# Where the decays' exponential is taken: per head from the broadcast row on ScalarE, with the causal mask moved to GpSimd

## What is computed

```python
log_fg = log_sigmoid(fgate)                      # gates come from q, k, v by a small matmul
cums = cumsum(log_fg);  fg_mat = cums[:, None] - cums[None, :]     # -inf above the diagonal
log_D = fg_mat + ig;    D = exp(log_D - max(log_D, -1))
C = (q @ k.T) / sqrt(128) * D
h = (C / (max(|sum(C)|, exp(-max_log_D)) + eps)) @ v               # then a norm per head
x = x + h * outnorm_weight
# feed-forward, BitNet style: act_quant(layernorm(x)) with ternary weights
x = x + bitlinear(silu(bitlinear(x, w_gate)) * bitlinear(x, w_up), w_down)
```

## Time and profile before

| | |
|---|---|
| median of 3 runs | 690.28 us (690.03 to 692.08) |
| span of the profiled execution | 685.3 us (its own time from launch to end is not given) |
| TensorE, VectorE busy | 85%, 83% of the span |
| ScalarE, GpSimd busy | 70%, 42% |
| mean granted clock of TensorE | 0.962 of full |

### The profile page before, as it was taken

The page is one execution under the profiler, slowest core; times in us unless marked ns, Lnnn a source line. Parts: engine busy times, 40 slices in busy tenths (PEclk is TensorE's granted clock), DMA queues, the critical chain, the costliest instruction groups (busy, mean ns, idle before and its releaser), DMA issues. The chain is left out here.

```text
span 685.3 us, 12637 instructions
## 1 busy us (share of the span) xinstructions
PE 579.8 (85%) x3568; PEld 377.8 (55%) x3630; DVE 567.8 (83%) x1518; ACT 476.5 (70%) x716; POOL 284.6 (42%) x459
## 2 busy tenths in 40 slices
PE   1824567889998999899998999799989999799996
PEld 1814555466555655476556656576537664456442
DVE  3149776889998998989899999899899889979863
ACT  1877766478866885678757885678667875865652
POOL 2015536624554444453543455444545256344200
PEclk9999756999999999999999999999999999999999
DMA  8852724101224102520242123310252031000001
GB/s 334 342 202 93 258 77 156 32 2 46 79 93 154 47 1 78 191 72 28 77 168 77 46 77 120 125 46 3 76 190 70 16 154 46 32 1 17 32 16 47
DMA packets 30753, 63.76 MB, mean 93 GB/s; under 512 B 2304, under 2 KB 18816, under 8 KB 27136
## 3 DMA queue, kind: packets, MB, share of 16 engines
q1 hardware_dynamic: 30144, 62.92, 25.4%
q10 hardware_dynamic: 576, 0.44, 0.3%
HBM read 54.84 MB, written 8.52 MB: 92 GB/s over the span
## 5 line engine op out<-in xcount | busy, mean ns | idle before, releaser
L558 PE MATMUL GU<-WQ,xqT 128*128 128x512 bf16 x977 | 240.3, 389 | 18.0 <-DVE FF L1161 15.4
L558 PEld LDWEIGHTS GU<-WQ,xqT 128*128 128x128 bf16 x1024 | 98.7, 100 | 121.5 <-DVE FF L1161 13.7
L588 PE MATMUL ACC<-WQ,FF 128*128 128x512 bf16 x497 | 115.0, 379 | 3.0 <-ACT FF L813 2.2
L794 ACT ACTIVATE FF<-GU,cgu 128x512 f32<-128x512 f32 x128 | 86.4, 688 | 24.5 <-PE GU L558 21.8
L1161 DVE TENSOR_TENSOR FF<-FF,GU 128x512 f32<-128x512 f32 x128 | 85.1, 680 | 8.5 <-ACT FF L794 5.5
L588 PEld LDWEIGHTS ACC<-WQ,FF 128*128 128x128 bf16 x512 | 49.6, 98 | 58.1 <-ACT FF L813 2.6
L802 ACT ACTIVATE FF<-FF,magic,hs 128x1024 f32<-128x1024 f32 x64 | 79.1, 1239 | 3.2 <-DVE hs L1192 3.2
L760 ACT ACTIVATE work<-AT,pb 128x128 f32<-128x128 f32 x128 | 47.9, 452 | 17.5 <-POOL pb L1450 16.4
L1457 POOL TENSOR_TENSOR work<-work,norm_bc 128x512 f32<-128x512 f32 x32 | 42.4, 1325 | 39.4 <-ACT work L760 39.4
L506 PE MATMUL AT<-vext,CT 128*128 128x129 f32 x256 | 54.1, 295 | 5.2 <-ACT gate_parts L699 3.8
L1412 POOL TENSOR_TENSOR qw<-qT,bc 128x512 f32<-128x512 f32 x32 | 46.0, 1448 | 19.6 <-DMA bc<-gate_rows 19.6
(11 more groups left out here) (116 smaller groups left out, 1187.7 us busy)
## 6 DMA issues: line engine op xcount, KB each, us to landing
bc<-gate_rows SPq DMA_DIRECT2D x8, 2048.0 KB, 7.4
xin<-in_x SPq DMA_DIRECT2D x32, 256.0 KB, 2.8
kT<-in_ctx_t SPq DMA_DIRECT2D x8, 1024.0 KB, 4.8
vext<-in_ctx SPq DMA_DIRECT2D x32, 256.0 KB, 3.4
out<-FF SPq DMA_DIRECT2D x32, 256.0 KB, 2.3
WQ<-in_w_gate SPq DMA_DIRECT2D x4, 1024.0 KB, 12.8
FF<-in_w_up SPq DMA_DIRECT2D x4, 1024.0 KB, 15.5
FF<-in_w_down SPq DMA_DIRECT2D x4, 1024.0 KB, 4.8
```

The source lines that it names most:

```text
L558: last = nc.tensor.matmul(dst, xqT[:, b, P * k:P * (k + 1)], w[:, k, 512 * j:512 * (j + 1)], start=(k == 0), stop=(k == KC - 1))
L588: last = nc.tensor.matmul(ACC[:, :], hT[:, b % 2, P * k:P * (k + 1)], WD[:, k, :], start=(k == 0), stop=(k == JT - 1))
L794: nc.scalar.activation(sg[:, j % 2, :], GU[:, 2 * (j % 2), :], ACT.Silu, scale=cgu[:, b, 0:1]).then_inc(silu_done, 1)
```

## The change

ScalarE's `exp_decay` no longer waits for an argument from VectorE. It waits for `cols` and `bc` themselves and takes four exponentials of 128x128, one per head, with the column as bias and scale -1. The mask leaves the argument: after ScalarE has copied the scores of the coming group, a new function `mask_scores` on GpSimd zeroes them above the diagonal, in place. Above the diagonal the exponential can now be huge, so `weigh` takes the minimum with 1 ahead of its product. `decay_argument` and the `mask` tile are gone. In GpSimd's queue the four masks of a body stand behind `x_rstd(coming, 3)`, `weigh_keys(now, 1)`, `weigh_q(now, 3)` and `x1_rstd(now, 0)`.

```diff
@@ scalar: exp_decay(g, b)
-                act.wait_ge(arg_done, g * 4 + (b + 1))
-                nc.scalar.activation(CT[:, NH * b:NH * (b + 1), :], CT[:, NH * b:NH * (b + 1), :], ACT.Exp,
-                                     scale=-1.0).then_inc(exp_done, 1)
+                n = g * 4 + b
+                cols_at, bc_in_at, num_done_at = values(act, g + 1, (g + 1) * 16, n - 3)
+                act.wait_ge(cols_ready, cols_at)
+                act.wait_ge(bc_in, bc_in_at)
+                if live(num_done_at):
+                    act.wait_ge(num_done, num_done_at)
+                for k in range(NH):
+                    r = NH * b + k
+                    last = nc.scalar.activation(CT[:, r, :], bc[:, r, 0, :], ACT.Exp, bias=cols[:, 0, r:r + 1], scale=-1.0)
+                last.then_inc(exp_done, 1)
@@ vector
-            def decay_argument(g, b):
...
-                    last = V.scalar_tensor_tensor(CT[:, r, :], bc[:, r, 0, :], cols[:, 0, r:r + 1], mask[:, :],
-                                                  ALU.subtract, ALU.max)
-                last.then_inc(arg_done, 1)
@@ vector: weigh(g, b)
-                dve.wait_ge(sc_ready, sc_ready_at)
+                dve.wait_ge(sc_masked, sc_masked_at)
...
-                V.tensor_tensor(CT[:, r, :], CT[:, r, :], scores[:, b, :].rearrange("p (h s) -> p h s", h=NH),
-                                ALU.mult).then_inc(ct_ready, 1)
+                V.scalar_tensor_tensor(CT[:, r, :], CT[:, r, :], 1.0, scores[:, b, :].rearrange("p (h s) -> p h s", h=NH),
+                                       ALU.min, ALU.mult).then_inc(ct_ready, 1)
@@ vector: iteration(it), four places
-                decay_argument(now, 0)
...
@@ gpsimd
+            def mask_scores(g, b):
...
+                sc_ready_at, = values(pool, g * 4 + (b + 1))
+                pool.wait_ge(sc_ready, sc_ready_at)
+                pool.sem_inc(pool_turn, 1)
+                G.affine_select(out=scores[:, b, :], in_=scores[:, b, :], compare_op=ALU.is_ge, fill=0.0, base=0,
+                                pattern=[[0, NH], [1, P]], channel_multiplier=-1).then_inc(sc_masked, 1)
@@ gpsimd: iteration(it)
                 x_rstd(coming, 3)
+                mask_scores(coming, 0)
                 weigh_q(now, 2)
                 weigh_keys(now, 1)
+                mask_scores(coming, 1)
                 head_scale(now, 0)
                 weigh_keys(now, 2)
                 weigh_q(now, 3)
+                mask_scores(coming, 2)
                 residual(now, 0, slot_now)
                 x1_rstd(now, 0)
+                mask_scores(coming, 3)
```

More of the change, by code:

```diff
@@ L54 @@
 FULL, FULL_END = 2, NG - 1
-NEVER = 1e30
 LOWEST = -3e38
@@ L111, in program @@
         ones = sb("ones", [P, P])
-        mask = sb("mask", [P, P])
         minus_half = sb("minus_half", [P, 8])
@@ L213, in program @@
         cols_ready = sem("cols_ready")
-        arg_done = sem("arg_done")
+        sc_masked = sem("sc_masked")
         exp_done = sem("exp_done")
@@ L1078, in weigh @@
                 n = g * 4 + b
-                sc_ready_at, exp_done_at = values(dve, n + 1, n + 1)
-                dve.wait_ge(sc_ready, sc_ready_at)
+                sc_masked_at, exp_done_at = values(dve, n + 1, n + 1)
+                dve.wait_ge(sc_masked, sc_masked_at)
                 dve.wait_ge(exp_done, exp_done_at)
                 r = slice(NH * b, NH * (b + 1))
-                V.tensor_tensor(CT[:, r, :], CT[:, r, :], scores[:, b, :].rearrange("p (h s) -> p h s", h=NH),
-                                ALU.mult).then_inc(ct_ready, 1)
+                V.scalar_tensor_tensor(CT[:, r, :], CT[:, r, :], 1.0, scores[:, b, :].rearrange("p (h s) -> p h s", h=NH),
+                                       ALU.min, ALU.mult).then_inc(ct_ready, 1)
             def head_stats(g, b):
@@ L1316, in iteration @@
                 x_stats(coming, 2, slot_coming)
-                decay_argument(now, 1)
                 x_norm(coming, 2, slot_coming)
@@ L1329, in iteration @@
                 x_norm(coming, 3, slot_coming)
-                decay_argument(now, 2)
                 if step == 0:
@@ L1339, in iteration @@
                 multiply(former, 2, 1)
-                decay_argument(now, 3)
                 result(former, 0, slot_former)
@@ L1413, in weigh_q @@
                                 ALU.mult).then_inc(qw_ready, 1)
+            def mask_scores(g, b):
+                if absent(g):
+                    return
+                sc_ready_at, = values(pool, g * 4 + (b + 1))
[3 more added lines that the diff above has]
+                                pattern=[[0, NH], [1, P]], channel_multiplier=-1).then_inc(sc_masked, 1)
             def weigh_keys(g, b):
@@ L1507, in _ @@
             G.memset(ident[:, :], 0.0).then_inc(pool_seq, 1)
-            G.memset(mask[:, :], 0.0).then_inc(pool_seq, 1)
             G.memset(ones[:, :], 1.0)
             G.memset(minus_half[:, :], -0.5)
-            pool.wait_ge(pool_seq, 2)
+            pool.wait_ge(pool_seq, 1)
             G.affine_select(out=ident[:, :], in_=ident[:, :], compare_op=ALU.not_equal, fill=1.0, base=0,
                             pattern=[[-1, P]], channel_multiplier=1).then_inc(pool_seq, 1)
-            G.affine_select(out=mask[:, :], in_=mask[:, :], compare_op=ALU.is_ge, fill=NEVER, base=0,
-                            pattern=[[1, P]], channel_multiplier=-1).then_inc(pool_seq, 1)
-            pool.wait_ge(pool_seq, 4)
+            pool.wait_ge(pool_seq, 2)
             G.tensor_copy(ident16[:, :], ident[:, :]).then_inc(pool_const, 1)
-            count.n = 4
+            count.n = 2
             for it in range(-1, FULL):
```

## The result

The changed kernel takes **715.41 us** at the median (710.9 to 717.73, 4 runs), against 690.15 (688.69 to 692.08) for the kernel before beside it: ratio **1.0365** (95% interval 1.0316 to 1.0415). A second set of runs on another chip gave 713.9 and 1.0327 (1.0271 to 1.0383). The forecast was 697.1 with a range up to 702.5: the sign was right, the loss is nearly four times as large. One edit, the place of one of the four masks in GpSimd's queue, turned out to cost some 32 us (some 30 by the second set); with that mask one step later the change is a gain of 1.0% (683.26 us). Two of the experiments (e3, e4) fell into a slower state of the clock in part of their executions; the comparisons leave those out, but the two profiles are of such executions.

The account below looks back on a forecast made before the run. VectorE and TensorE, both nearly full, bound each body where one stands still for the other. Terms -12.0 + 4.9 + 15.4 - 1.5 = +6.8 us on 690.3 gave 697.1 us, range 683.5 to 702.5.

Parts of the forecast that it names:

- The turn: From VectorE's x_norm(coming, 1) to the first numerator matmul: 15.1 us shortens to 12.7 in five bodies, -12.0 us.
- the bound of -7: Smallest saving allowed for the turn, in us, if it keeps a clock drop in every second body.
- exp(now, 2) on the path: ScalarE's longer exponential ahead of TensorE's state_step delays it 0.7 us in bodies 1 to 7: +4.9 us.
- weigh: VectorE's weigh as scalar_tensor_tensor costs 0.07 us more each, with nobody waiting: 0, bounds -1 and +3.
- the mask's price: One GpSimd mask of 128x512 takes 0.59 us, bounds 0.29 and 1.18.
- The x1 chain: Score copy, batch-2 mask, residual, then VectorE's x1_stats: the mask's wait delays x1_stats 2.2 us in seven bodies, +15.4 us.
- the slack rival: VectorE's shed work lets it run ahead, so x1_stats is off the path: 681.7 us, faster; chance 0.24.
- So a delay of x1_stats goes straight to TensorE, and the rest of the body (...) hands it on: From x1_stats through transpose_h(former, 2, 1) to the body's end, a delay passes on unchanged; no extra time counted.
- a rival only for the masks' own reads: Masks' memory reads hold up VectorE's two-input instructions 0.59 us in eight bodies: 4.7 us, 701.8; counted within the dear case.
- the dear case: Mask takes 1.18 us (+4.2) and TensorE's x1 wait lowers the clock in three of seven bodies (+4.2): 705.5; chance 0.12.
- First and last passes: First regains ScalarE's 2.2 us wait for arguments, last pays for longer exponentials: together -1.5 us, bounds -4 and +2.
- Median and span: Span 685.3 against median 690.28: some 5 us lie around the span and don't change.

Follow-up runs that it names:

- e3: Kernel before, with only a wait for the copy of score(coming, 2) added in GpSimd's queue ahead of residual(now, 0), no mask; ratio 1.0433.
- e4: Kernel before, with the four masks added at the changed kernel's places in GpSimd's queue, arguments and single exponential kept; ratio 1.0523.
- e1: Changed kernel, with the batch-2 mask moved behind residual(now, 0) in GpSimd's queue; 683.26 us, ratio 0.9899.
- e5: Changed kernel, with GpSimd's residual(former, 1) also waiting for VectorE's x_norm(coming, 0); 699.04 us, ratio 1.0112.
- e2: Changed kernel without any masks, weigh waiting for the score copy instead; 683.91 us, ratio 0.9902.
- e6: Changed kernel with the batch-2 mask behind residual(now, 0), and residual(former, 1) also waiting for x_norm(coming, 0); 686.14 us, ratio 0.9899.
- e7: Kernel before, arguments kept, with four 128x128 exponentials with a bias column of zeros instead of one of 128x512; 698.2 us, ratio 1.0114.
- a2: The one kept busy: changed kernel, 8 extra TensorE matmuls per body ahead of its wait at transpose_h; 713.13 us, again 713.28 beside 713.9 unchanged.

## Why the prediction was right and wrong

Right was the mechanism and its sign: the wait of one mask, ahead of the residual, outweighs what the turn gains. By its steps:

**The turn** (forecast 12.7 us, saving 12.0 over the five loop bodies). Without a fall of the clock it is 12.4 us: ScalarE is the late one, as said, and no 2.42 us wait of TensorE is left. In the second profile the five save 12.8 us (75.5 to 62.7). In the first they save 6.5, under the bound of -7: two of them took 15.95 and 15.74. The step that failed is "TensorE's one long idle time in it is gone, so I count no clock drop". An idle time of 1.1 us stays, and falls still come there in some executions.

**exp(now, 2) on the path** (+0.7 each). It is on the path, at +0.43 each: +2.6 for +4.9. The line of the exponentials in the changed kernel, with minimum, median and maximum in ns:

```profile
L742 ACT ACTIVATE CT<-bc,cols x128: 384/389/408, 56.9 to 627.5; 128x128 f32<-128x128 f32 x128
```

Four take 1.27 to 1.28 us for 1.33 forecast, so the size was near; 0.2 us of the delay was absorbed on the way to state_step.

**weigh** (0) and **the mask's price** (0.59, bounds 0.29 and 1.18):

```profile
L1075 DVE SCALAR_TENSOR_TENSOR CT<-CT,scores x32: 673/693/1486, 61.3 to 629.5; 128x512 f32<-128x512 f32 x32
...
L1410 POOL TENSOR_SCALAR_AFFINE_SELECT scores<-scores x32: 635/642/855, 21.2 to 564.0; 128x512 f32<-128x512 f32 x32
```

The new weigh has the old one's least time, 673 against 672 ns, and its median fell from 1038 to 693. The mask takes 0.64 us, near the 0.59 built from the small one. (By the Trainium skill's figure, GPSIMD Engine Reference, section 3.1, the prediction had estimated 0.77; the measured 0.64 decides.) Both were well priced.

**The x1 chain** (+2.2 each, +15.4). x1_stats is 2.5 us later per middle body: the two hand-overs are 401.18 - 401.01 = 0.17 and 404.77 - 404.56 = 0.21 us where I had 0.12 for both. In bodies 1 to 6 this sums to +15.9, and to +19.0 with body 0; the ends cost more (3.1 in body 0, 3.3 in body 6), where the old distance was under 1 us. The step was right and so was the rejection of the slack rival: 3.17 us less of VectorE work per turn bought nothing against a wait that begins at a product of TensorE's. The time of that rival, 681.7 us, is nearly that of e1 (683.26), where the chain is undone, so the rest of the sum was about right as a whole.

**"So a delay of x1_stats goes straight to TensorE, and the rest of the body (...) hands it on"** is the step that failed, with +8.3 and +4.8 us that the sum had at nothing. The delay wasn't handed on, it grew. I treated the stretch from x1_stats to transpose_h as rigid, because VectorE is full there. It is full, but with instructions whose length depends on what GpSimd does at that moment. VectorE came 2.5 us later and GpSimd 2.06, and the 0.44 us between them put three VectorE instructions behind GpSimd's where one had been before: +1.8 us (e3, e4 show it without any other part of the change, e5 takes it away). The prediction knew the effect, 345 ns against 1399, and put it into a rival only for the masks' own reads, which e2 shows to be free. Behind the longer wait at transpose_h, 3.2 us instead of 1.0, the clock then fell in three of five bodies. That was in the dear case, at 4.2 us with a chance of 0.12; it came at 4.8, beside a cheap mask.

**First and last passes** (-1.5). They came to +4.0 us, of which +3.1 is the x1_stats of body 0, counted above; so without it about +1, inside its bounds.

**Median and span.** The prediction put 5 us around the span; the profiled execution of after took 717.73 us with a span of 716.0, so 1.7 lie around it. The profiled execution of before was thus some 3 us faster than its median. For the difference this matters little.

Together, over the 6.8 forecast: +5.5 for the turns of it 2 to 6 and +1.5 for that of it 1, -2.3 for state_step, +3.6 for the x1 chain (19.0 for 15.4), +8.3 for the meetings, +4.8 for the clock behind transpose_h, +2.4 for the passes at both ends. That is 30.6 of the 30.7 us between the spans; in the second profile of the changed kernel the turns take 6.8 less and the difference is 23.4.

**What stays open.** The changed kernel and the one kept busy show that the falls move when a wait is filled, and e6 shows that they can come back where a stretch gets shorter. What one fall costs in the end, if every other were held fixed, no run isolates. e7's turns got 4.5 us longer in six bodies; 3.6 of these are in it 1 and it 4, whose clock falls were shorter or absent before, and in e7's profile all five turns of it 2 to 6 have a fall, where four had one before. So the longer exponentials themselves show little in the turns, but no run holds the clock fixed to say how much.

## What to carry to other kernels

Before an instruction that waits is put into an in-order queue, look at what stands behind it and at who reads that; place it behind the last urgent item, even where it could run earlier. When a delay enters a stretch that is full, don't assume that it is handed on at its own size: lay the other engine's timeline beside it, work out by how much each of the two is shifted, and look whether their order turns round: here 0.44 us turned it round, and a small VectorE instruction behind a large one of GpSimd's was held until that was nearly done. And an engine's share of busy time, 83 to 74% here, says nothing of what relief of it is worth.

## What the runs showed of the hardware

- A scan of 16x128 on VectorE takes 0.47 us alone and 1.31 beside a GpSimd tensor_tensor of 128x512; a tensor_tensor of 16x128 takes 0.28 and 1.34; a tensor_scalar of 128x512, with one input and two columns, 0.53 and 1.32. Smallness is no protection; the order is: the same scan, started 0.08 to 0.10 us ahead of GpSimd's instruction, kept its 0.47 us, and started 0.32 to 0.35 us behind it, took 1.31. The other way round, GpSimd's second instruction took 1.56 us where VectorE's x_norm had started 0.11 us ahead of it, and 1.27 otherwise.
- GpSimd's affine_select of 128x512 f32, in place, takes 0.64 us, 0.60 from its start to the next instruction's; of 128x128 it took 0.29.
- Four activations of 128x128 with bias column take 1.28 us where one of 128x512 without took 0.63. The Trainium skill (ScalarE: Activation LUTs, section "What ACT_TABLE_LOAD costs") gives 280 ns + 0.833 ns per element with an overlap of 93 ns; by that estimate four take 3 x 0.294 + 0.387 = 1.27 us, and the trace agrees.
- A wait of TensorE of 3.2 us was followed by the lower clock level in three of five bodies, one of 1.1 us in the turn in some; filling the former (a2) or shortening it (e5) moved the falls to the latter, and with the filling the time stayed within 0.2%.
